# Heads in pairs on the two halves of the array, in a kernel of chunked, latent and expert layers on one core

## The reference

```python
xn = _layernorm(x)
# branch 1: attention within chunks of 16 tokens, once on neighbours, once on every third token
q = heads(_linear(xr, Wq, bq)); k = heads(_linear(xr, Wk, bk)); v = heads(_linear(xr, Wv, bv))
attn = softmax(einsum('bhqd,bhkd->bhqk', q, k) * SCALE)
out = einsum('bhqk,bhkd->bhqd', attn, v)
branch1 = _linear(local_out + atrous_out, Wo, bo)
# branch 2: causal attention over 512 tokens with low-rank q, k, v and rotary halves, then experts
y = xn + mla(rmsnorm(xn, w_ln1), ...)     # 16 heads, scores (512 x 512), causal, softmax, @ W_o
xt = rmsnorm(y, w_ln2)
shared = silu(xt @ Wg_s) * (xt @ Wu_s) @ Wd_s
# 7 routed experts, the two with the highest sigmoid(logits) weighted, all computed
combined = einsum('tei,eih,te->th', silu(xt @ Wg_r) * (xt @ Wu_r), Wd_r, wts)
result = x + branch1 + y + shared + combined
```

## Time and profile before

| | |
|---|---|
| median of 3 runs | 498.77 us (498.15 to 499.48) |
| span of the profiled execution | 498.5 us |
| TensorE busy | 438.1 us (88%) |
| VectorE busy | 364.8 us (73%) |
| ScalarE busy | 264.8 us (53%) |
| POOL busy | 63.9 us (13%) |
| moved by DMA | 20.05 MB, 40 GB/s |

### The profile page before, as it was taken

The page is one execution under the profiler, slowest core; times in us unless marked ns, Lnnn a source line. Parts: engine busy times, 40 slices in busy tenths (PEclk is TensorE's granted clock), DMA queues, the critical chain, the costliest instruction groups (busy, mean ns, idle before and its releaser), DMA issues.

```text
span 498.5 us, 10894 instructions
## 1 busy us (share of the span) xinstructions
PE 438.1 (88%) x4044; PEld 232.8 (47%) x4044; DVE 364.8 (73%) x1049; ACT 264.8 (53%) x486; POOL 63.9 (13%) x56
## 2 busy tenths in 40 slices
PE   2667569899999999999999997899998999987995
PEld 2323233345445356354545544454545545654653
DVE  6566288388767887796768785667687775788886
ACT  5236247545876663778865375776543444221110
POOL 7233002433000220110002030000010000010000
PEclk9997599899999999999999998999999999999898
DMA  6037300016600124700001355000400000000000
GB/s 202 9 75 157 43 2 2 3 34 151 103 3 3 34 46 88 122 3 2 3 2 22 71 122 75 3 3 2 130 1 3 2 1 23 1 21 1 1 21 22
DMA packets 21124, 20.05 MB, mean 40 GB/s; under 512 B 2856, under 2 KB 19752, under 8 KB 20680
## 3 DMA queue, kind: packets, MB, share of 16 engines
q1 hardware_dynamic: 21072, 19.36, 18.7%
HBM read 10.70 MB, written 7.47 MB: 36 GB/s over the span
## 4 chain that ended last, share of the span: by engine, by line
PE 52%; DVE 27%; issue 7%; DMA 5%; ACT 4%; SPq 3%; POOL 1%; DVEq 0%; ACTq 0%; POOLq 0%
PE bank_A L1071 7%; PE bank_c L1034 6%; PE bank_A L1000 6%; PE bank_B L1020 5%; PE bank_M L1082 5%; DVE x L943 4%; DMA q_stack<-in_c_rows 4%; DVE k_diag L923 4%; DVE k_diag L928 3%; PE bank_B L1115 3%; PE bank_M L986 3%; PE bank_M L1089 2%; DVE differences L819 2%; SPq L468 2%; PE bank_A L1121 2%
## 5 line engine op out<-in xcount | busy, mean ns | idle before, releaser
L672 ACT ACTIVATE p_mla<-bank_B 128x512 f32<-128x512 f32 (+1 forms) x176 | 97.4, 561 | 78.9 <-PE bank_B L1023 77.1
L819 DVE CUSTOM_DVE_ANT_0 differences<-masks,bank_A 128x384 bf16<-128x384 bf16 (+1 forms) x128 | 78.4, 612 | 18.7 <-PE bank_A L1000 13.4
L651 ACT ACTIVATE pT_loc<-sT_loc 32x512 f32<-32x512 f32 x136 | 85.1, 625 | 4.5 <-DVE sT_loc L846 3.1
L1000 PE MATMUL bank_A<-k_stack,q_stack 128*128 128x128 bf16 (+3 forms) x256 | 70.1, 307 | 14.5 <-DMA q_stack<-in_c_rows 8.0
L1020 PE MATMUL bank_B<-q_stack,k_stack 128*128 128x512 bf16 (+3 forms) x256 | 67.9, 302 | 1.0 <-DVE k_diag L923 0.8
L1115 PE MATMUL bank_B<-xrT,k_diag 128*128 128x512 f32 x128 | 63.7, 612 | 3.7 <-DVE k_diag L923 3.2
L839 DVE TENSOR_REDUCE row_max<-bank_A 128x16 f32<-128x512 f32 (+1 forms) x36 | 24.8, 690 | 39.4 <-PE bank_A L1071 39.2
L1071 PE MATMUL bank_A<-k_diag,qT 128*32 128x512 f32 x272 | 49.7, 757 | 0.0
L1023 PE MATMUL bank_B<-masks 128*128 128x128 bf16 x256 | 49.1, 219 | 0.0
L1000 PEld LDWEIGHTS bank_A<-k_stack,q_stack 128*128 128x128 bf16 x256 | 25.6, 100 | 49.9 <-issue 26.4
L1034 PE MATMUL bank_c<-p_mla,v_mla 128*9 128x128 f32 (+3 forms) x512 | 47.0, 437 | 1.4 <-ACT p_mla L672 1.4
(11 more groups left out here) (137 smaller groups left out, 624.8 us busy)
## 6 DMA issues: line engine op xcount, KB each, us to landing
parts_dram<-parts SPq DMA_DIRECT2D x16, 192.0 KB, 2.7
k_stack<-parts_dram SPq DMA_DIRECT2D x8, 384.0 KB
q_stack<-parts_dram SPq DMA_DIRECT2D x8, 384.0 KB
parts_dram<-parts SPq DMA_DIRECT2D x16, 128.0 KB, 2.7
k_diag<-kT SPq DMA_DIRECT2D x64, 18.0 KB
x<-in_x SPq DMA_DIRECT2D x4, 256.0 KB, 7.6
parts_dram<-parts SPq DMA_DIRECT2D x16, 64.0 KB, 2.3
out<-x SPq DMA_DIRECT2D x4, 256.0 KB, 2.2
```

What stands on the lines that cost most here:

```text
L651: last = nc.scalar.activation(pT_loc[rows, :, rows], sT_loc[rows, t % 2, :].rearrange("p (h k) -> p h k", h=H), ACT.Exp, scale=SCALE)
L672: drained_by(nc.scalar.activation(p_mla[:, n % P_RING, m:m + len(heads), j * P:], src, ACT.Exp, scale=SCALE), step)
L819: drained_by(nc.vector.tensor_tensor_reduce(differences[:, 0:w], masked16[:, S - w:], bank[:, 0:w], -1.0, -NEG, ALU.add, ALU.min, dst), step)
L1000: last = nc.tensor.matmul(bank[:, n * w:(n + 1) * w], q_stack[b % 2][:, h // 2, h % 2, i * P:(i + 1) * P], k_stack[b % 2][:, h // 2, 0:w], ...
```

## The change

The layout of the stacks: a head takes 54 of 64 rows (48 of terms, 4 of query tile indicators, 2 of shift). Heads 0 to 7 lie in rows 0 to 63 and heads 8 to 15 in rows 64 to 127. S and E contract over one half. E of a group runs beside S of the group two places further on (`LEAD = 2`), and TensorE issues the two matmul by matmul, in bank B and bank A. The causal masks of both are matmuls of 64 rows and 64 columns a head, and four constant rows mask the rest of a block; VectorE's custom maximum becomes a plain reduction.

The stacks are filled by copies from SBUF to SBUF, one for each term and half (`to_stack`), and the shifts likewise.

Local attention works on units of eight pairs of chunks (five a batch): `k_diag` holds two sets of eight heads by 16 keys, the exponential is one instruction (LR), a new step PT turns the probabilities by TensorE, and ScalarE writes them into the block-diagonal `pT_loc` in six copies. The values are laid out block-diagonally through DRAM (VD), LO writes its result with tokens in rows, and LY is gone.

MB is one matmul for queries and keys. ScalarE drains DOWN with the expert's weight and POOL adds it to x, except for the last one. Matmuls on the identity are added at the start (`WARM`). All steps but the first batch's projections are merged by one new table. The core of the diff:

```diff
-    "latent": [(0, 1.12), (1.12, 2.02), (2.02, 2.86), (2.86, 4)],
+    "scores": [(-0.544, 4.136)],
+    "local": [(-0.436, 0.411), (0.765, 1.39), (1.708, 2.786), (2.68, 3.494)],
...
+    def scores():
+            here = groups[n] if n < len(groups) else None
+            back = groups[n - LEAD] if n >= LEAD else None
+            exps = [("E",) + back + (j, u) for j in range(NT) for u in range(len(exp_units(back[1], j)))] if back else []
+            for k in range(PER_GROUP):
+                unit = []
+                if here:
+                    unit.append(("S", here[0], PER_GROUP * GROUP_ORDER.index(here[1]) + k))
+                if back:
+                    unit.append(exps[k])
+                found.append(unit + late + (shift if k == 1 else []))
+                late = []
+                if back and (k + 1 == PER_GROUP or exps[k + 1][3] != exps[k][3]):
...
+        steps = [("VD", b, 0)]
+        for k in range(NLU + 1):
+            if k < NLU:
+                steps.append(("LS", b, k))
+            if k == NLU - 1:
+                steps += [("KD", b + 1, n) for n in range(KD_PARTS)] if b + 1 < B else [("WX",)]
+            if k:
+                steps.append(("LO", b, k - 1))
+                if k == LOCAL_UNITS:
+                    steps.append(("VD", b, 1))
+            if k < NLU:
+                steps += [("LR", b, k), ("PT", b, k)]
+            if k:
+                steps.append(("LT", b, k - 1))
...
+        def to_stack(eng, b, side, part, hp):
+            stack = (q_stack if side else k_stack)[b % 2]
+            for term in TERMS_OF[side][part]:
+                rows = slice(SLOT * hp + term, SLOT * hp + QUAD_ROW, TERMS)
+                eng.dma_start(stack[rows, :, :], parts[hp::2, side, part, :]).then_inc(stacks_in[b % 2][hp], 16)
...
+                if step == ("ST", 0, 0):
+                    for side, part in ((0, 0), (0, 1), (0, 2), (1, 1), (1, 2)):
+                        if part < 2:
+                            sp.wait_ge(rounded[side], part + 1)
+                        else:
+                            sp.wait_ge(split_ready, side + 1)
+                        to_stack(sp, 0, side, part, 0)
+                if kind == "ST2":
...
+                    row, a0 = SLOT * (g // 2) + SHIFT_ROW, 4 * (g % 2)
+                    for r in range(2):
+                        sp.dma_start(q_stack[b % 2][row + r:row + r + 1, a0:a0 + 4, :].rearrange("o a (i n) -> o (a i) n", n=P),
+                                     shift[:, r, :]).then_inc(shift_in[g], 16)
...
+                if step[0] == "DOWN" and step != final:
+                    _, c, e = step
+                    tb = slice(c * NT, (c + 1) * NT)
+                    if e == 0:
+                        pool.wait_ge(summed, c + 1)
+                    wait_drained(pool, step)
+                    link(nc.gpsimd.tensor_tensor(x[:, tb, :], x[:, tb, :], weighted[down_no[step] % 2], ALU.add))
+                    pool.sem_inc(added, 1)
...
-                    for j in range(len(LTILES[step[2]])):
-                        rows = slice(PAIR * j, PAIR * j + PAIR)
-                        last = nc.scalar.activation(pT_loc[rows, :, rows],
-                                                    sT_loc[rows, t % 2, :].rearrange("p (h k) -> p h k", h=H),
-                                                    ACT.Exp, scale=SCALE)
...
+                    nc.scalar.activation(p_loc[0:np_, 0:w], s_loc[0:np_, 0:w], ACT.Exp, scale=SCALE).then_inc(loc_exp, 1)
...
+                    for top in range(2):
+                        rows = slice(SLOT * top, SLOT * top + SLOT)
+                        to = pT_loc[rows, t % PT_RING]
+                        nc.scalar.copy(view(to[:, top, 0, 0:], (P, 2 * tiles), (PAIR, np_), (1, CHUNK)),
+                                       view(bank[rows, 0:], (P, 2 * tiles), (PAIR, np_), (1, CHUNK)))
+                        for g in range(2):
+                            ins = nc.scalar.copy(
+                                view(to[:, 1 - top, g, CHUNK:], (2 * P, tiles), (PAIR, np_), (1, CHUNK)),
+                                view(bank[rows, P * (1 - g) + CHUNK:], (2 * P, tiles), (PAIR, np_), (1, CHUNK)))
...
+                    down = bank[:].rearrange("p (i d) -> p i d", i=NT)
+                    if e == 0:
+                        ins = nc.scalar.activation(weighted[n % 2], down, ACT.Copy, scale=0.5)
+                    else:
+                        for i in range(NT):
+                            ins = nc.scalar.activation(weighted[n % 2][:, i, :], down[:, i, :], ACT.Copy,
+                                                       scale=expert_w[:, c * NT + i, e - 1:e])
+                    drained_by(ins, step)
...
-                        drained_by(nc.vector.tensor_tensor_reduce(differences[:, 0:w], masked16[:, S - w:],
-                                                                  bank[:, 0:w], -1.0, -NEG, ALU.add, ALU.min, dst), step)
-                    else:
-                        dst = neg_max[:, g, :, a0:a0 + len(heads) // 2, i].rearrange("p e a -> p a e")
-                        src = src.rearrange("p (a e) k -> p a e k", e=2)
-                        drained_by(nc.vector.tensor_reduce(dst, src, AX.X, ALU.max, negate=True), step)
+                    g, m = heads[0] // 4, heads[0] % 4
+                    drained_by(nc.vector.tensor_reduce(neg_max[:, g, m:m + len(heads), i], src, AX.X, ALU.max, negate=True), step)
...
-                    nc.vector.transpose(sT_loc[0:np_, t % 2, :], s_loc[0:np_, :]).then_inc(loc_turned, 1)
...
-                elif kind == "DOWN":
...
-                    for i in range(NT):
-                        t = c * NT + i
-                        weight = 0.5 if e == 0 else expert_w[:, t, e - 1:e]
-                        ins = nc.vector.scalar_tensor_tensor(out=x[:, t, :], in0=down[:, i, :], scalar=weight,
-                                                             in1=x[:, t, :], op0=ALU.mult, op1=ALU.add)
...
+            def half_of(h):
+                return slice(SLOT * (h // 8), SLOT * (h // 8) + SLOT)
+
+            def maxima_matmul(step, n):
+                b, (i, heads) = step[1], UNITS[step[2]]
+                h, w = heads[n], (i + 1) * P
+                rows = slice(half_of(h).start, half_of(h).start + SHIFT_ROW)
+                return nc.tensor.matmul(bank_of(step)[:, n * w:(n + 1) * w],
+                                        q_stack[b % 2][rows, h % 8, i * P:(i + 1) * P],
+                                        k_stack[b % 2][rows, h % 8, 0:w], start=n == 0, stop=False,
+                                        skip_group_check=True)
+
+            def mask(to, heads, low, triangle):
+                half = half_of(heads[0])
+                return nc.tensor.matmul(to, half_eye[half, low, :],
+                                        triangle[half, :].unsqueeze(1).broadcast_to((SLOT, len(heads), SLOT)),
+                                        start=False, stop=True, skip_group_check=True)
+
...
+                    other = beside.get(step)
+                    for m in range(len(exp_units(g, j)[u])):
+                        exp_matmul(step, m)
+                        if other:
+                            maxima_matmul(other, m)
+                    for low in range(2):
+                        done = exp_mask(step, low)
+                        if other:
+                            last = maxima_mask(other, low)
+                    full_by(done, step)
+                    if other:
+                        full_by(last, other)
...
-                    nc.tensor.matmul(bank[0:np_, :], eye16[:, 0:np_], pair16, start=True, stop=False, skip_group_check=True)
-                    for j, (_, first, stp) in enumerate(LTILES[step[2]]):
-                        last = nc.tensor.matmul(bank[PAIR * j:PAIR * j + PAIR, :], qT[:, b % 2, tokens(first, stp)],
-                                                k_diag[:, :, tokens(first, stp)], start=False, stop=True,
-                                                skip_group_check=True)
...
+                    pairs = LUNITS[step[2]][0]
+                    for t in range(loc_tiles(step)):
+                        for a in range(2):
+                            for j, pair in enumerate(pairs[4 * t:4 * t + 4]):
+                                c = 2 * P * t + P * a
+                                last = nc.tensor.matmul(bank[PAIR * j:PAIR * j + PAIR, c:c + P], q_part[:, a, pair, :],
+                                                        k_diag[:, a, :, CHUNK * pair:CHUNK * pair + CHUNK],
+                                                        start=True, stop=True, skip_group_check=True)
...
+                elif kind == "PT":
+                    t, np_ = loc_no(step), loc_rows(step)
+                    pe.wait_ge(loc_exp, t + 1)
+                    for c in range(2 * loc_tiles(step)):
+                        last = nc.tensor.transpose(bank[:, P * c:P * c + np_], p_loc[0:np_, P * c:P * c + P],
```

(14 more changed lines are left out.)

976 lines of the change are left out of this document (587 added, 389 removed).

## The result

The changed kernel takes **393.26 us** (median of three executions, 389.66 to 394.65) where the kernel before took 498.77: a ratio of 0.787, 95% interval 0.782 to 0.793. A second set of executions gave 392.51 (388.87 to 396.61), ratio 0.780 (0.777 to 0.783). The forecast was 380, its range 352 to 425. The profile shown is that of the 389.66 us execution; its span is 387.9 us.

What follows compares the result with a forecast made beforehand. TensorE was taken to bound the scores and local attention, VectorE the experts' pace. Start 28, sixteen groups of scores 242, last two groups 13, experts 93, final sums and store 4 sum to 380 us; range 352 to 425.

Steps and rivals of the forecast that it cites:

- The start: Stage up to the first score matmul: 28 us, or 35 were each copy within SBUF twice as slow.
- The pairs: S and E matmuls on TensorE in different halves of the array: full overlap, 49 us, a saving of 41 us.
- Rival 1: Score stage: the halves don't overlap, TensorE gets 48 us more there, 422 us in all; chance 0.12.
- The middle: Sixteen groups of scores: TensorE and VectorE nearly equally loaded in one hand-set order, 242 us, a load of 90%.
- The experts: Expert stage: TensorE sets the pace at 2.62 us an expert; 93 us with other matmuls, ports and late picks.
- GpSimd's hold on VectorE: Norms and picks of the expert stage: POOL instructions slow VectorE's between SBUF tensors, charged 4 us.
- Rival 2: SP's queue: the copies bind, shifts late by 5 us in each batch, start at 33, 405 us; chance 0.12.
- Rival 4: Matmuls of 64-row tiles: their weights aren't hidden and nothing overlaps, 552 us, slower than before; chance 0.03.
- Rival 3: Score stage as dense as the earlier middle, 233 us, start at 25, outputs 6 less: 362 us; chance 0.12.
- Last two groups: Groups without scores beside them: ScalarE's exponentials set them at 6.7 us each, 13 us.
- A change of mode: TensorE's array mode changes 356 times instead of 303: 0.1 us charged for each of 53 more, 5 us.
- The local outputs: Local attention on TensorE: 544 output matmuls of 36 columns, between 15 and 30 us, taken as 22, saving 16.

Runs made afterwards that it cites:

- pv_later: Changed kernel with the products with the values for key tiles 0 and 1 of a group one score unit later: 393.2 us, ratio 0.786.
- local_twice: Changed kernel with every round of local score matmuls issued twice into the same place, VectorE's work unchanged: 406.6 us, ratio 0.812.
- half_maxima: Changed kernel with the reductions of the scores reading only the first half of each unit's keys: 387.8 us, ratio 0.775.
- tiny_same: Changed kernel with one extra single-column matmul ahead of each of 176 E steps, in E's own 64-row tile: 391.4 us, ratio 0.784.
- tiny_other: Changed kernel with the 176 extra single-column matmuls of tiny_same, but over 128 rows, so the array's mode changes more often: 398.8 us, ratio 0.799.
- best: Changed kernel with the edits of half_maxima and pv_later and the S side's masks left out: 391.3 us, ratio 0.783.

## Why the prediction was right, and where it was off

**Right by its own steps.** The start: 28 forecast, first score matmul at 28.79; with the GpSimd memset gone the four LayerNorm instructions take 1.12 us (5.33 in the earlier trace rows), and the six issues of keys took 4.05 us. The pairs: full overlap, next pair after 0.22 us, TensorE's total 337.9 where 341 was forecast. Rival 1 is refuted by the trace. The run with both in one half took 420 us, where rival 1 said 422, but that agreement is luck: it is 27 us above the changed kernel, with some of it the clock, and rival 1 had added 42 to 380. The middle: 245.1 for 242, at a load of 87% for 90%. The experts: 2.62 us where undisturbed, as worked out from the earlier trace rows. GpSimd's hold on VectorE: 5 us for 4. Rival 2: E waits for the shifts' copy once, for 1.1 us; dead. Rival 4: no load of weights shows between the two starts of a pair; dead. Rival 3 needed 14 us of idle TensorE in the middle; there are 32.

**The step that failed** is the term that said: "**Last two groups** have no scores beside them: ScalarE's exponentials set them", 13 us. They took 21.3 us, the whole of the sum's 7.9 us surplus and a little more. The timeline of the changed kernel, products with the values (PV) of one of these groups:

```profile
277.59 1.06 PE L1332 MATMUL bank_c<-p_mla,v_mla 128*32 128x512 f32 x8 [0.19 <-ACT p_mla L886]
...
280.33 0.85 PE L1332 MATMUL bank_c<-p_mla,v_mla 128*32 128x384 f32 x8 [0.26 <-ACT p_mla L886]
...
282.30 0.64 PE L1332 MATMUL bank_c<-p_mla,v_mla 128*32 128x256 f32 x8 [0.24 <-ACT p_mla L886]
...
283.25 0.43 PE L1332 MATMUL bank_c<-p_mla,v_mla 128*32 128x128 f32 x8
...
291.59 1.99 PE L1428 MATMUL bank_B<-xrT,k_diag 128*128 128x512 f32 x4
```

A group without scores beside it has 3.0 us of PV and, by the distances of the earlier trace rows, 3.1 us of E with masks, 0.65 for the turns of Y and some eight changes of mode, at 0.05 each: 7.2 us of TensorE, more than ScalarE's 6.7. And two experts' first products (2 x 1.95 us, the last row) are merged into the stage, which takes that work out of the next one. The prediction did give TensorE 12 us for the two groups, about what E and PV make, and so found ScalarE above it; the turns, the changes of mode and the experts' products were missing. TensorE's 7.2 twice and the 3.9 are 18.3 us, TensorE is idle for 1.7 more, and 1.3 I can't assign. The experts' stage is shorter by that 3.9, and measured 88.3 where 93 was forecast. Both stages together: 106 forecast, 109.6 measured. The order of PV is the smaller part of the miss: pv_later moved it, and the stage took 19.9 us, with TensorE busy for 19.45 of them.

**Terms that were off and cancelled.** I let all 16 groups of S and of E overlap, 49 us together; with E two groups behind only 14 of each stand beside one another, so by the same prices (3 us a group) 6 us were missing. A change of mode costs 0.02 to 0.05 us of time, not 0.1: 53 more are 1 to 3 us, not 5. The local outputs took 14.5 us for 22, at the low bound. The local scores show 21.4 us busy for 15; the extra matmuls of local_twice put their price at 15.9. VectorE is busy for 286.0 us, not 271. By stages it is 23.0 for 17 at the start, where some 3 us are the copies that lay out the small weights and 2.6 the first batch's masked keys, which I had put on ScalarE; 197.9 for 193 in the middle, and 65.1 for 61 behind it. None of it set the time, as half_maxima shows for the middle. ScalarE has 224 us, not 240: copies into blocks and drains cost 62 us instead of 72, and the rest was small.

**And the last 5 us.** I took the profiled span for the median within 0.3 us, as it was for the kernel before. For this kernel it isn't: 387.9 against 393.3. Between the two executions that were profiled such a difference is stretches of lower clock in a stage that TensorE now bounds. I had named no term for it.

## What to carry to other kernels

Where the contraction is at most 64 rows, two streams in different halves of the array and different banks run at the price of one, and they needn't be written in turn: it was enough that the partner stood within three matmuls. To find a bound between two engines that are both 80 to 90% busy, change the load of each by itself: here 41 us less on VectorE gave 3 to 6 us, 16 more on TensorE cost 14. Where two versions differ by a few us, match the starts of the same instructions in both traces before naming a cause: of the 9.7 us between the profiled executions of tiny_same and tiny_other, 4.4 came in two steps where the clock was lower. For a stage with a single stream left, add up every engine's work in it, not only the one that waits in the trace.

## What the runs showed of the hardware

- Matmuls of different halves of the array start out of program order: S starts 0.01 us behind E, ahead of up to three matmuls of the other half that stand before it.
- A change of mode: 0.08 to 0.1 us between starts; 0.02 to 0.03 us of time at the same clock, 0.05 with the clock's share.
- GpSimd's additions beside VectorE's instructions between SBUF tensors cost VectorE 5 us: four casts of 128 x 32 took 1.8 us with them and 0.7 without.
- Small edits move the mean granted clock: 0.962 to 0.989 in the changed kernel, 0.957 to 0.978 without S's masks, 0.961 to 0.976 with PV later, 0.952 to 0.964 in best. Why isn't shown.
- One stretch at the lower clock costs 1.7 to 1.8 us in the stage that TensorE bounds and 0.9 to 1.2 before 80 us. That makes the whole 4.9 us between the two profiled executions; the others of the spread from 389 to 397 us weren't profiled.
